# A decoder's nine layer norms fed without their centring product, after output weights and biases are centred once on the chip

## The chip, the cores and the metric

The kernel runs on one core of one Trainium2 chip. The metric is the device time of one launch in microseconds. Five engines work on a core, each with its own queue in program order: TensorE (PE, matrix products into the accumulation memory PSUM), VectorE (DVE), ScalarE (ACT), GpSimd (POOL) and SyncE (SP, which here issues the transfers). They wait for one another through semaphores.

## The reference, cut to what matters

32 sequences of 128 tokens with 128 features, and for each a context of 77 rows with 64 features, pass through a decoder of four levels (L0 to L3). A level has self attention, cross attention to the context, and a feed-forward part (a mixture of experts, a small linear map, or a stack of attention and MLP layers). The norm after each part is

```python
def _layernorm(x, axis=-1, eps=1e-05):
    m = jnp.mean(x, axis=axis, keepdims=True)
    v = jnp.var(x, axis=axis, keepdims=True)
    return (x - m) / jnp.sqrt(v + eps)
```

and it is applied to the sum of the part's input and its output: `x = norm(x + attention(x) @ Wo + bo)`. Some inner norms have a gain and a shift as well. The map of `L2_ffn` has a ternary weight: each element of W is rounded to -s, 0 or s by the mean absolute value s of W. In cross attention of L0 and L3 there is one head and no output matrix: the output is `softmax(q k) v`, with `v = ctx @ Wv + bv`.

## The kernel before, in words

All is kept transposed: a tile is 128 features (on the partitions) by 512 columns, four sequences of 128 tokens, f32. A loop of four turns takes a *group* of 8 sequences, as two *chains* (c = 0 and 1) of four. Ahead of the loop is a setup: SP loads the small weights (one tile `small`), POOL makes masks and identities, DVE makes `center` (the identity minus 1/128) and `average` (1/128), an output bias for two of the attentions, and the ternary weight `tern`; two small products on PE serve it (lines 429 to 465).

A norm (29 in a group, for each of the two chains) is a chain of six steps, and since the features lie on the partitions, a mean over them needs a matrix product:

1. `centre`, line 549, PE: `center` times the residual sum, into a PSUM bank: x minus its mean.
2. `square`, line 982, ACT: the square of that bank, into `sq` in SBUF.
3. `variance`, line 557, PE: `average` times `sq`, into another bank.
4. and 5. `inverse_deviation`, lines 991 and 994, ACT: logarithm of the variance plus eps, then exp(-0.5 of it), into `part`.
6. `apply`, lines 1229 to 1243, DVE: the centred bank times `part`, and gain and shift where there are any.

A product of f32 tiles is two instructions on PE, so a count of products is half of the count in a row.

The order of work is written out by hand on each engine. Between two stages lie the norms. The generator `front` yields after each part of a norm and after each part of the next stage's head (its first products); `crossing` advances the generators of the two chains in turn, and the stages call `step(second)` and `step(then)` at fixed places in their own bodies. So in the last item of self attention (`mha`, item t = 9) the first chain's centring product is issued ahead of the last `attend` (line 731 or 721), and its variance product behind it, ahead of the second chain's output product (line 753). After cross attention (`xattn`) and after the linear map (`linear`) both chains do their norms together (`close`).

PSUM has eight banks. `Banks.take` hands them out from rings, each ring in turn: `flow` goes round all eight, `scores` banks 0 to 3, `turned` and `head` 4 and 5, `attend` 6, `wide` 7. Whoever takes a bank waits for the event named as `freed_by` by the tenant before it. A centred tile frees its bank when the norm is applied, a variance tile when its logarithm is taken. `norm_rings` says from which rings a norm takes its two banks: in front of self attention the second chain's centred tile gets `attend` and its variance `wide`, and a first norm of the first chain gets `flow`, or `scores` after self attention.

`warm(n)`, line 542, issues n products without use, 128x512 in bf16, that keep PE at work in places where it would idle. Line 601 are the q and k products of a self attention head, 784 those of cross attention, 859 the router's logits, 829, 876 and 883 the first products of MLP and experts, 846 and 910 the second ones, 938 the product with `tern`.

Of the kernel before, what the change touches and what calls it, by code (L numbers as in the profile page):

```python
# [14 lines left out]
ALU = mybir.AluOpType  # L15
ACT = mybir.ActivationFunctionType
AX_X = mybir.AxisListType.X

P = 128
BATCH = 32  # L20
CTX_LEN, CTX_DIM = 77, 64
# [82 lines left out]
def sequence():  # L104
# [3 lines left out]
    seq = []  # L108

    def norm(name, src, after, dst, **k):  # L110
        seq.append(dict(kind="norm", name=name, src=src, after=after, dst=dst, eps=1e-5, g=None, add=None, behind=None) | k)
        return ("normed", name)
# [22 lines left out]
    e = norm("L0_xattn_ln", "u", e, "x")  # L135
    e = moe("L0_ffn", "x", e, shared=True, act=ACT.Gelu_apprx_tanh, glu=False, on="logits")
    e = norm("L0_ffn_ln", "u", e, "x")
    for i in range(DEPTH):
        n = f"L1_{i}"
        y = "x" if i == 0 else "y"  # L140
        e = norm(n + "_ln1", y, e, "hn", g=n + "_ln1")
# [7 lines left out]
    e = norm("L1_xattn_ln", "u", e, "x")  # L149
# [3 lines left out]
    e = norm("L2_attn_ln", "u", e, "x")  # L153
    e = norm("L2_ln1", "x", e, "y", g="L2_ln1")
# [14 lines left out]
    e = norm("L2_ffn_ln", "u", ("residual", "L2_ffn"), "x")  # L169
    e = mha("L3_attn", "x", e, "x", "u", mask="far", rel=True, bias=True, bo="L3_attn_bo",  # L170
            wiped="L2_a2")
    e = norm("L3_attn_ln", "u", e, "x")
    e = xattn("L3_xattn", e)
    e = norm("L3_xattn_ln", "u", e, "x")
    e = mha("L3_ffn", "x", e, "x", "u", bo="L3_ffn_bo")
    e = norm("L3_ffn_ln1", "u", e, "y", g="L3_ffn_ln1", eps=1e-6)
# [104 lines left out]
def decoder(nc, io, known):  # L281
# [17 lines left out]
    with ExitStack() as ctx:  # L299
# [32 lines left out]
        const_v = sb("const_v", [P, 2])  # L332
        out_bias = {n: sb("out_bias_" + n, [P, 1]) for n in ("L2_attn", "L3_attn")}
# [53 lines left out]
        setup_step = ctx.enter_context(nc.semaphore("setup_step"))  # L387
        setup_sum = ctx.enter_context(nc.semaphore("setup_sum"))

        with nc.Block() as block:  # L390
# [32 lines left out]
            def _(dve):  # L423
# [7 lines left out]
                nc.vector.memset(average[:], 1.0 / P)  # L431
                nc.vector.memset(average64[:], 1.0 / CTX_DIM)
# [13 lines left out]
                link(nc.vector.tensor_tensor(const_v[:, 1:2], W("L3_rel_v")[:, 0:1], W("L3_attn_bv"), ALU.add))  # L446
                dve.wait_ge(setup_sum, 2)
                for i, n in enumerate(out_bias):
                    nc.vector.tensor_tensor(out_bias[n][:], psum[1][:, i:i + 1], W(n + "_bo"), ALU.add)
# [5 lines left out]
                nc.vector.tensor_tensor(tern[:], tern[:], tern_neg[:], ALU.subtract)  # L455

            @block.tensor
            def _(pe):
# [4 lines left out]
                pe.wait_ge(setup_step, 5)  # L463
                for i, n in enumerate(out_bias):
# [56 lines left out]
        with nc.Fori(0, BATCH // GROUP) as g:  # L521
            with nc.Block() as block:

                @block.tensor
                def _(pe):
# [19 lines left out]
                    def centre(st, c, ring):  # L545
                        n, rows, w = st["name"], st.get("rows", P), st.get("cols", TOK)
                        pe.wait_ge(*input_of(st["after"], c))
# [422 lines left out]
                def _(act):  # L970
# [8 lines left out]
                    def square(st, c):  # L979
                        n, rows, w = st["name"], st.get("rows", P), st.get("cols", TOK)  # L980
                        act.wait_ge(*have("centred", (n, c)))
# [873 lines left out]
```

## Time and profile before

| | before |
|---|---|
| median of 3 runs | 5704.05 us (5701.13 to 5717.39) |
| the profiled execution's own time | 5674.14 us |
| its span in the profile | 5672.6 us |
| mean granted PE clock | 0.962 |
| PE busy | 5110.4 us, 90% |
| PE weight loads | 2613.1 us, 46% |
| ACT busy | 3051.5 us, 54% |
| DVE busy | 2829.6 us, 50% |
| POOL busy | 23.6 us, 0% |
| transfers | 15 GB/s in the mean |

The profile is of one execution, 30 us shorter than the median of the runs. Its four turns of the loop take 1405 to 1420 us each and repeat one pattern, so one group is read closely and multiplied by four. Busy time of PE is modelled at its ends and holds the filler products. An idle time in a row, in brackets, names what ended it.

### The profile page before, as it was taken

To read this page: it belongs to the slowest core of one execution; us is meant where nothing else is said; L and a number is where in the kernel's file an instruction comes from. 1 tells how busy PE (TensorE), PEld (TensorE's weight loads), DVE (VectorE), ACT (ScalarE), POOL (GpSimd) and SP (SyncE) were. 2 spreads that over 40 slices of the span, in tenths; PEclk is the share of its full clock that TensorE was granted. 3 is DMA by queue.
4 is the path that set the end of the run, shared out by engine and by line. 5 is a ranking of instruction groups with operands and counts; after the bars stand their busy time and mean duration, and the time that the engine had idled before them with its cause. 6 is when DMAs were issued, how large, how long until landed. Compare 5 with 4: busy or idle time off the path is not lost. (4 is left out here: it accounts for less than half of the span.)

```text
span 5672.6 us, 81045 instructions
## 1 busy us (share of the span) xinstructions
PE 5110.4 (90%) x27990; PEld 2613.1 (46%) x27990; DVE 2829.6 (50%) x6564; ACT 3051.5 (54%) x11252; POOL 23.6 (0%) x34
## 2 busy tenths in 40 slices
PE   7999988889799998888889999888898999989889
PEld 4444445544444444554344444455434444445443
DVE  5255555562525555556253545555625255555562
ACT  5444565564544456656454445665645444466564
POOL 0000000000000000000000000000000000000000
PEclk9989999999999999999999989999999999999999
DMA  1100000000010000000001000000000100000000
GB/s 37 41 6 6 18 18 12 5 1 15 25 41 6 6 21 18 9 5 1 19 25 37 6 6 20 18 9 5 1 19 22 41 6 6 23 16 9 5 1 19
DMA packets 22511, 85.93 MB, mean 15 GB/s; under 512 B 2512, under 2 KB 3024, under 8 KB 21968
## 3 DMA queue, kind: packets, MB, share of 16 engines
q1 hardware_dynamic: 22096, 80.58, 4.4%
q8 instruction: 238, 3.90, 0.3%
q14 instruction: 177, 1.45, 0.1%
HBM read 78.47 MB, written 2.10 MB: 14 GB/s over the span
## 5 line engine op out<-in xcount | busy, mean ns | idle before, releaser
L1051 ACT ACTIVATE work<-bank,rowmax 128x128 f32<-128x128 f32 (+1 forms) x4096 | 1395.1, 395 | 306.7 <-DVE rowmax L1366 305.9
L1051 ACT ACTIVATION_READ_ACCUMULATOR work<-bank,rowmax 128x1 f32 x4096 | 989.1, 244 | 0.0
L1366 DVE TENSOR_REDUCE rowmax<-bank 128x4 f32<-128x512 f32 (+2 forms) x1152 | 610.8, 578 | 458.8 <-PE bank L677 346.6
L694 PE MATMUL bank<-ident,work 128*128 128x128 f32 (+1 forms) x4096 | 658.2, 289 | 134.5 <-DVE probsT L1425 101.9
L542 PE MATMUL bank<-mask_causal,identb 128*128 128x512 bf16 x2368 | 676.3, 394 | 40.1 <-issue 28.7
L694 PEld LDWEIGHTS bank<-ident,work 128*128 128x128 f32 (+1 forms) x4096 | 488.6, 148 | 349.1 <-DVE probsT L1425 172.5
L1164 ACT ACTIVATE work<-bank,small 128x512 f32<-128x512 f32 x544 | 371.8, 688 | 490.1 <-PE bank L883 490.1
L910 PE MATMUL bank<-work,slot 128*128 128x512 f32 x1344 | 611.7, 592 | 0.0
L1621 DVE SCALAR_TENSOR_TENSOR part<-bank,small,sq 128x512 f32<-128x512 f32 x192 | 144.1, 751 | 785.0 <-PE bank L910 775.4
L1425 DVE COPY probsT<-bank 128x512 f32<-128x512 f32 (+2 forms) x832 | 479.6, 600 | 68.7 <-PE bank L694 64.9
L677 PE MATMUL bank<-km,q 32*128 32x512 f32 (+2 forms) x1792 | 426.2, 570 | 19.3 <-ACT work L1051 11.9
L910 PEld LDWEIGHTS bank<-work,slot 128*128 128x128 f32 x1344 | 254.7, 190 | 294.5 <-issue 288.7
L542 PEld LDWEIGHTS bank<-mask_causal,identb 128*128 128x128 bf16 x2368 | 224.7, 101 | 270.4 <-issue 151.7
L991 ACT ACTIVATE part<-bank,eps 128x512 f32<-128x512 f32 (+1 forms) x232 | 157.5, 679 | 334.7 <-PE bank L557 334.2
L982 ACT ACTIVATE sq<-bank 128x512 f32<-128x512 f32 (+1 forms) x232 | 136.9, 590 | 363.0 <-PE bank L549 362.6
L731 PE MATMUL bank<-probsT,vm 128*32 128x128 f32 (+1 forms) x6144 | 273.3, 286 | 49.4 <-ACT probsT L1065 36.6
L731 PEld LDWEIGHTS bank<-probsT,vm 128*32 128x32 f32 (+1 forms) x6144 | 188.1, 113 | 201.8 <-issue 154.0
L883 PE MATMUL bank<-x,slot 128*128 128x512 f32 x576 | 265.2, 603 | 0.0
L1076 ACT ACTIVATE spreadT<-bank 128x128 f32<-128x128 f32 (+3 forms) x352 | 138.1, 392 | 228.0 <-PE bank L707 228.0
L557 PE MATMUL bank<-sq,average 128*128 128x512 f32 (+1 forms) x464 | 249.0, 627 | 12.1 <-DVE x L1229 8.7
L876 PE MATMUL bank<-x,slot 128*128 128x512 f32 x512 | 239.4, 609 | 21.5 <-DVE work L1609 21.5
L883 PE MATMUL bank<-y,slot 128*128 128x512 f32 x512 | 235.7, 601 | 7.2 <-ACT work L1164 7.2
(266 smaller groups left out, 6226.6 us busy)
## 6 DMA issues: line engine op xcount, KB each, us to landing
slot<-in_w_stream SPq DMA_DIRECT2D x68, 512.0 KB, 3.4
slot<-in_w_stream SPq DMA_DIRECT2D x32, 768.0 KB, 3.9
slot<-in_w_stream SPq DMA_DIRECT2D x32, 384.0 KB, 3.1
small<-in_w_small SPq DMA_DIRECT2D x1, 2288.0 KB, 9.0
x<-in_x SPq DMA_DIRECT2D x8, 256.0 KB, 3.6
out<-x SPq DMA_DIRECT2D x8, 256.0 KB, 2.0
ctx<-in_ctx SPq DMA_DIRECT2D x8, 77.0 KB, 3.4
```

The costliest lines, as they stand in the source:

```text
L542: nc.tensor.matmul(b[:], identb[:], mask["causal"][:].unsqueeze(1).to_broadcast([P, 4, P]), start=True, stop=True)
L557: nc.tensor.matmul(b[0:rows, 0:w], (average if rows == P else average64)[:], B["sq"][c][0:rows, 0:w], start=True, stop=True).then_inc(*mad ...
L677: nc.tensor.matmul(banks.where(("scores", n, c, s, r))[:, 0:J * nk], B["q"][c][g32, s * P:(s + 1) * P], km[c][g32, s, 0:J, 0:nk], start=no ...
L694: ins = nc.tensor.transpose(b[0:nk, j * P:(j + 1) * P], probs[t % 2][:, r, j, 0:nk], ident[:])
L731: ins = nc.tensor.matmul(b[g32, 0:P], vals[c][0:nk, s, j, g32], pr[0:nk, r, j, :], start=(j == 0), stop=(j == J - 1))
L876: nc.tensor.matmul(b[:, 0:TOK], W(f"{base}_{w}_{e}")[:, m * P:(m + 1) * P], src, start=True, stop=True).then_inc(*made(lab, (n, e, c, m)))
L883: nc.tensor.matmul(b[:, 0:TOK], W(f"{base}_W1_{e}")[:, m * P:(m + 1) * P], src, start=True, stop=True).then_inc(*made("hid_raw", (n, e, c, ...
L910: ins = nc.tensor.matmul(b[:, 0:TOK], w[:, m * P:(m + 1) * P], hid[c][:, m, :], start=(m == 0), stop=(m == M - 1))
L1051: ins = nc.scalar.activation(probs[t % 2][:, r, j, 0:nk], banks.where(("scores", n, c, s, r))[:, j * nk:(j + 1) * nk], ACT.Exp, bias=rowma ...
L1164: nc.scalar.activation(hid[c][:, m, :], banks.where(("hid_raw", n, e, c, m))[:, 0:TOK], st["act"], bias=W(base + "_b1")[:, 4 * e + m:4 * e ...
L1366: V.tensor_reduce(m[:, 4 * r:4 * r + J], banks.where(("scores", n, c, s, r))[:, 0:J * nk] .rearrange("p (j k) -> p j k", j=J), AX_X, ALU.m ...
L1425: ins = V.tensor_copy(out, raw)
```

## The change

Six output matrices (the value matrix in the two cross attentions that have no output matrix) and five biases are centred over the output features in the setup: the mean of each row of the weight is subtracted on DVE, and the biases are multiplied by `center` on PE. Five products with one column each and the wait for the weights stand ahead of the two that were there. The ternary weight is centred as well. After that the sum of a normed x and such an output has mean zero over the features before it is normed. Nine of the 29 norms are marked `centred`: `L0_xattn_ln`, `L1_0_ln1`, `L1_xattn_ln`, `L2_attn_ln`, `L2_ln1`, `L2_ffn_ln`, `L3_attn_ln`, `L3_xattn_ln` and `L3_ffn_ln1`. For these `centre` issues nothing and takes no bank, `square` reads the residual sum in SBUF as soon as it is written, and `apply` multiplies from SBUF. `L1_0_ln1` and `L2_ln1` take the output of the norm just before. The other 20 norms are as they were. The yields stay, so the places of all other instructions do too.

```diff
-    e = norm("L0_xattn_ln", "u", e, "x")
+    e = norm("L0_xattn_ln", "u", e, "x", centred=True)
...
+        centred_weights = ["L0_xattn_Wv", "L1_xattn_Wo", "L2_attn_Wo", "L3_attn_Wo", "L3_xattn_Wv", "L3_ffn_Wo"]
+        centred_biases = ["L2_attn_bo", "L3_attn_bo", "L0_xattn_bv", "L3_xattn_bv", "L3_ffn_bo"]
+        wmean = sb("wmean", [P, len(centred_weights) + 1])
...
+                nc.vector.memset(wmean[:], 0.0)
...
                 link(nc.vector.tensor_tensor(const_v[:, 1:2], W("L3_rel_v")[:, 0:1], W("L3_attn_bv"), ALU.add))
+                for i, name in enumerate(centred_weights):
+                    rows = CTX_DIM if name.endswith("Wv") else P
+                    ins = nc.vector.tensor_reduce(wmean[0:rows, i:i + 1], W(name, rows), AX_X, ALU.add)
+                link(ins)
+                link(nc.vector.tensor_scalar(wmean[:, 0:len(centred_weights)], wmean[:, 0:len(centred_weights)], 1.0 / P,
+                                             None, ALU.mult))
+                for i, name in enumerate(centred_weights):
+                    rows = CTX_DIM if name.endswith("Wv") else P
+                    ins = nc.vector.tensor_scalar(W(name, rows), W(name, rows), wmean[0:rows, i:i + 1], None, ALU.subtract)
+                ins.then_inc(weights_centred, 1)
                 dve.wait_ge(setup_sum, 2)
+                for i, name in enumerate(centred_biases):
+                    ins = nc.vector.tensor_copy(W(name), psum[2][:, i:i + 1])
+                link(ins)
...
-                nc.vector.tensor_tensor(tern[:], tern[:], tern_neg[:], ALU.subtract)
+                link(nc.vector.tensor_tensor(tern[:], tern[:], tern_neg[:], ALU.subtract))
+                link(nc.vector.tensor_reduce(tcol[:, 0:1], tern[:], AX_X, ALU.add))
+                link(nc.vector.tensor_scalar(tcol[:, 1:2], tcol[:, 0:1], 1.0 / P, None, ALU.mult))
+                nc.vector.tensor_scalar(tern[:], tern[:], tcol[:, 1:2], None, ALU.subtract)
...
                 pe.wait_ge(setup_step, 5)
+                pe.wait_ge(weights_centred, 1)
+                for i, name in enumerate(centred_biases):
+                    nc.tensor.matmul(psum[2][:, i:i + 1], center[:], W(name), start=True, stop=True)
                 for i, n in enumerate(out_bias):
...
                     def centre(st, c, ring):
                         n, rows, w = st["name"], st.get("rows", P), st.get("cols", TOK)
+                        if st["centred"]:
+                            return
...
-                        act.wait_ge(*have("centred", (n, c)))
-                        nc.scalar.activation(B["sq"][c][0:rows, 0:w], banks.where(("centred", n, c))[0:rows, 0:w],
+                        act.wait_ge(*(input_of(st["after"], c) if st["centred"] else have("centred", (n, c))))
+                        src = B[st["src"]][c] if st["centred"] else banks.where(("centred", n, c))
+                        nc.scalar.activation(B["sq"][c][0:rows, 0:w], src[0:rows, 0:w],
                                              ACT.Square).then_inc(*made("squared", (n, c)))
...
-                        cen = banks.where(("centred", n, c))[0:rows, 0:w]
+                        cen = (B[st["src"]][c] if st["centred"] else banks.where(("centred", n, c)))[0:rows, 0:w]
```

## Rows read from the trace of the kernel before

**Rows 1.** The page, part 1: busy time, share of the span and instructions of each engine.

```profile
PE 5110.4 (90%) x27990; PEld 2613.1 (46%) x27990; DVE 2829.6 (50%) x6564; ACT 3051.5 (54%) x11252; POOL 23.6 (0%) x34
```

**Rows 2.** Who waited for whom: engine, tile and line, releaser, us in total, times, longest.

```profile
ACT sq L982 <- PE bank L549: 362.6, 216, 4.6
```

**Rows 3.** Timeline of the setup: start us, us, engine line op out<-in xcount [idle before <-releaser].

```profile
10.49 0.28 DVE L442 TENSOR_REDUCE tcol<-small 128x1 f32<-128x128 f32 x1
...
11.33 1.01 PE L465 MATMUL bank<-const_v,small 128*128 128x1 f32 x4
```

**Rows 4.** Timeline of `L0_xattn_ln` of group 0, both chains.

```profile
122.86 2.09 PE L549 MATMUL bank<-u,center 128*128 128x512 f32 x4
...
124.03 0.60 ACT L982 ACTIVATE sq<-bank 128x512 f32<-128x512 f32 x1 [2.27 <-PE bank L549]
```

**Rows 5.** Timeline of the tail of `L3_ffn`, group 0.

```profile
1280.83 1.02 PE L549 MATMUL bank<-u,center 128*128 128x512 f32 x2
...
1280.92 0.60 ACT L1065 ACTIVATE probsT<-bank 128x512 f32<-128x512 f32 x1 [5.49 <-PE bank L694]
...
1281.87 1.08 PE L731 MATMUL bank<-probsT,vm 128*32 128x128 f32 x32
```

**Rows 6.** Timeline of `L1_xattn_ln`, group 0, second chain's centring product and what follows it.

```profile
629.86 0.68 DVE L1229 TENSOR_TENSOR x<-bank,part 128x512 f32<-128x512 f32 x1
...
630.96 0.95 PE L859 MATMUL bank<-small,x 128*128 128x8 f32 x8
```

**Rows 7.** Timeline of `L2_attn_ln` and `L2_ln1`, group 0.

```profile
814.52 0.60 ACT L982 ACTIVATE sq<-bank 128x512 f32<-128x512 f32 x1 [1.54 <-PE bank L549]
...
816.40 0.69 ACT L991 ACTIVATE part<-bank,eps 128x512 f32<-128x512 f32 x1 [0.42 <-PE bank L557]
...
822.37 0.69 ACT L991 ACTIVATE part<-bank,eps 128x512 f32<-128x512 f32 x1 [0.26 <-PE bank L557]
```

**Rows 8.** Timeline of the start of `L1_0`, group 0, first chain's q and k.

```profile
272.76 1.93 PE L601 MATMUL bank<-hn,slot 128*64 128x512 f32 x4
```

**Rows 9.** Timeline of `L2_ffn_ln` and the start of `L3_attn`, group 0.

```profile
1077.62 0.69 DVE L1647 TENSOR_TENSOR u<-bank,x 128x512 f32<-128x512 f32 x1 [2.17 <-PE bank L938]
...
1083.07 1.12 PE L557 MATMUL bank<-sq,average 128*128 128x512 f32 x2 [2.16 <-DVE x L1229]
...
1084.89 1.88 PE L601 MATMUL bank<-x,small 128*128 128x512 f32 x4
```

**Rows 10.** Timeline of `L1_3_ln2`, group 0.

```profile
542.00 0.49 DVE L1243 TENSOR_SCALAR hn<-hn,small 128x512 f32<-128x512 f32 x1
...
542.63 1.95 PE L549 MATMUL bank<-y,center 128*128 128x512 f32 x2 [2.12 <-DVE hn L1243]
```

**Rows 11.** Timeline of `L1_attn_ln`, group 0, second chain, and the head of `L1_xattn`.

```profile
563.86 1.12 PE L549 MATMUL bank<-u,center 128*128 128x512 f32 x2 [0.71 <-DVE u L1532]
...
565.69 1.02 PE L601 MATMUL bank<-x,small 128*128 128x512 f32 x2
```

**Rows 12.** Timeline of `L2_a2_ln3`, group 0, TensorE alone.

```profile
1050.19 1.98 PE L829 MATMUL bank<-hn,slot 128*128 128x512 f32 x4
```

**Rows 13.** Windows: us, busy us (xcount) of the five engines, granted clock, DMA share, GB/s.

```profile
266.60:321.80 55.20, 50.64 (x266) 27.44 (x267) 34.70 (x111) 22.92 (x92) 0.00 (x0) 0.81 0.01 3
488.80:537.60 48.80, 43.30 (x270) 23.52 (x268) 34.36 (x112) 21.42 (x90) 0.00 (x0) 1.00 0.03 9
1194.80:1198.00 3.20, 1.09 (x4) 0.26 (x3) 1.17 (x2) 2.04 (x6) 0.00 (x0) 1.00 0.03 5
1198.00:1208.50 10.50, 10.36 (x31) 6.32 (x32) 3.86 (x9) 2.23 (x7) 0.00 (x0) 0.51 0.00 0
```

**Rows 14.** Lines by shape: engine op operands xcount | busy us, mean ns | idle before.

```profile
L994 ACT ACTIVATE part<-part 128x512 f32<-128x512 f32 x224 | 141.0, 630 | 7.2
...
L982 ACT ACTIVATE sq<-bank 128x512 f32<-128x512 f32 x224 | 133.6, 596 | 356.1 <-PE bank L549 356.1
...
L1627 DVE TENSOR_TENSOR u<-u,part 128x512 f32<-128x512 f32 x152 | 105.2, 692 | 5.2
```

More of the change, by code:

```diff
@@ L110, in norm @@
     def norm(name, src, after, dst, **k):
-        seq.append(dict(kind="norm", name=name, src=src, after=after, dst=dst, eps=1e-5, g=None, add=None, behind=None) | k)
+        seq.append(dict(kind="norm", name=name, src=src, after=after, dst=dst, eps=1e-5, g=None, add=None, behind=None,
+                        centred=False) | k)
         return ("normed", name)
@@ L140, in sequence @@
         y = "x" if i == 0 else "y"
-        e = norm(n + "_ln1", y, e, "hn", g=n + "_ln1")
+        e = norm(n + "_ln1", y, e, "hn", g=n + "_ln1", centred=i == 0)
         e = mha(n, "hn", e, y, "y", D=16, mask="causal", linear=True, bo=n + "_bo")
@@ L148, in sequence @@
     e = mha("L1_xattn", "x", e, "x", "u", nk=CTX_LEN, kv="ctx", kv_after=("ctx_loaded", ""))
-    e = norm("L1_xattn_ln", "u", e, "x")
+    e = norm("L1_xattn_ln", "u", e, "x", centred=True)
     e = moe("L1_ffn", "x", e, shared=False, act=ACT.Silu, glu=True, on="logits")
@@ L152, in sequence @@
     e = mha("L2_attn", "x", e, "x", "u", mask="causal", bias=True, bo="L2_attn_bo")
-    e = norm("L2_attn_ln", "u", e, "x")
-    e = norm("L2_ln1", "x", e, "y", g="L2_ln1")
+    e = norm("L2_attn_ln", "u", e, "x", centred=True)
+    e = norm("L2_ln1", "x", e, "y", g="L2_ln1", centred=True)
     e = norm("L2_a1_lnx", "y", e, "hn", g="L2_a1_lnx", g2="L2_a1_lny", dst2="hn2")
@@ L168, in sequence @@
     seq.append(dict(kind="linear", name="L2_ffn", src="x", after=e))
-    e = norm("L2_ffn_ln", "u", ("residual", "L2_ffn"), "x")
+    e = norm("L2_ffn_ln", "u", ("residual", "L2_ffn"), "x", centred=True)
     e = mha("L3_attn", "x", e, "x", "u", mask="far", rel=True, bias=True, bo="L3_attn_bo",
             wiped="L2_a2")
-    e = norm("L3_attn_ln", "u", e, "x")
+    e = norm("L3_attn_ln", "u", e, "x", centred=True)
     e = xattn("L3_xattn", e)
-    e = norm("L3_xattn_ln", "u", e, "x")
+    e = norm("L3_xattn_ln", "u", e, "x", centred=True)
     e = mha("L3_ffn", "x", e, "x", "u", bo="L3_ffn_bo")
-    e = norm("L3_ffn_ln1", "u", e, "y", g="L3_ffn_ln1", eps=1e-6)
+    e = norm("L3_ffn_ln1", "u", e, "y", g="L3_ffn_ln1", eps=1e-6, centred=True)
     e = moe("L3_ffn_moe", "y", e, shared=False, act=ACT.Gelu, glu=False, on="probs")
@@ L387, in decoder @@
         setup_step = ctx.enter_context(nc.semaphore("setup_step"))
+        weights_centred = ctx.enter_context(nc.semaphore("weights_centred"))
         setup_sum = ctx.enter_context(nc.semaphore("setup_sum"))
```

## The prediction

> **What bounds the kernel now.** I began with the page's busy shares [rows 1]: TensorE (PE) is busy 90% of the span, DVE and ACT about half. That doesn't make every matmul worth its time. Many PE instructions are fillers on L542, and each norm is a chain in which the engines take turns: residual (DVE), centring product (PE), square (ACT), variance product (PE), logarithm and exponential (ACT), multiplication (DVE). The list of waits shows the link that the change cuts: ACT waited 362.6 us in 216 instances for L549 [rows 2], 1.68 us each. 72 of the 232 centring products go (9 norms x 2 chains x 4 groups). By that mean they would be worth 121 us, but most chains run in pairs, or behind other work. So I read the nine places in the timeline one by one, in group 0, for what ends last, and used the windows for PE's granted clock.
>
> **The setup** is ahead of the loop and nothing covers it. Now two one-column products take 1.01 us and a 128x128 reduction 0.28 us [rows 3]. Added: six reductions, one small scaling, six subtractions on DVE, then five more products behind the last of them, five small copies, and a reduction, a scaling and a subtraction on the ternary weight. Products: 5 x 0.5 = 2.5 us. DVE pieces, each between 0.15 (overlapped) and 0.28 us: 13 before the products, 8 after, 3.1 to 5.9 us. Together 5.6 to 8.4 us; I take 6.1, near the lower end, since independent DVE instructions overlap. Once per run.
>
> **The centring product on the path**, per group. A product of this shape starts 122.86 and its square at 124.03 [rows 4]: 1.17 us from written input to square, which now starts at once.
> - `L0_xattn_ln` and `L3_xattn_ln`: both chains run together behind cross attention, so the pair saves one latency: 1.2 each, 2.4.
> - Four norms follow self attention (`L1_xattn_ln`, `L2_attn_ln`, `L3_attn_ln`, `L3_ffn_ln1`). There the first chain's product sits in PE's queue ahead of the last attend: 1280.83, attend at 1281.87, while the probabilities it needs are ready at 1280.92 + 0.60 = 1281.52 [rows 5]. Saved 0.3 in each. In the second chain nothing waits for its square, which is early, but the next stage's first product is queued behind the centring: x is ready at 629.86 + 0.68 = 630.54, the product starts 630.96 [rows 6]: 0.4 more in `L1_xattn_ln` and, by the same pattern, in `L3_attn_ln` (0.5). Without `L2_attn_ln`: 0.7 + 0.8 + 0.3 = 1.8.
> - `L2_attn_ln` with `L2_ln1`: the second chain's square is at 814.52, the two logarithms that follow in turn at 816.40 and 822.37 [rows 7]. The square can start when u is written, 1.2 earlier, and 0.3 from the tail; its variance no longer queues behind the first chain's second centring, nor does `L2_ln1`'s. I get 814.7 and 820.6 for the logarithms: 1.8, of which the 0.3 is part.
> - `L1_0_ln1`: q and k start at 272.76 [rows 8], behind the second chain's centring and four fillers; without it the variances go 0.6 earlier and hn is ready at 272.0: 0.75.
> - `L2_ffn_ln`: here a PSUM bank decides. The second variance (1083.07) waits 2.16 us until DVE has normed the first chain [rows 9], because its bank was last the first chain's centred tile. That tile is gone. u of the second chain is written at 1077.62 + 0.69 = 1078.31; square, the first chain's logarithm (0.69), exponential (0.63) and multiplication (0.69) end at 1081.1, and q starts there instead of 1084.89: 3.8 here, 4.0 to 4.1 where the first variance ran late too. I take 4.0.
>
> Sum of these: 2.4 + 1.8 + 1.8 + 0.75 + 4.0 = 10.75 us.
>
> **Banks that rotate.** The rings hand out banks in turn, so every dropped take shifts all later ones. I counted the takes of a group through. One wait goes: `L1_3_ln2` of the second chain starts its centring at 542.63, only after hn of the first is done at 542.49 [rows 10]; without it the products behind start 0.9 earlier. Two come. The second centring of `L1_attn_ln` (563.86) lands in the bank of the first and waits for its norm, 565.3; q, now at 565.69 [rows 11], comes behind it and four fillers, at 567.0: +1.35. The second centring of `L2_a2_ln3` waits in the same way until hn is ready, and the products of 1050.19 [rows 12] come 0.9 later. Bounds: 0, where the bank is free in time, and 2.2, two latencies. Net +1.35 per group.
>
> **The clock.** PE's granted clock was 1.00 in 1194.8 to 1198.0, with PE busy 1.09 of 3.2 us, and 0.51 in the next 10.5 us [rows 13]: it falls to the lower level, 1.2 GHz of 2.4, after little work. The change takes work out of such places. By my working new stretches without a full matmul arise ahead of `L1_0` (2.4 us), `L1_xattn` (2.3), the router of `L1_ffn` (2.3), in `L2_ln1` (3.3), before `L2_a2_mlp` (2.1) and before `L3_ffn_moe` (3.1, only 8-column products in it); two go, at `L1_3_ln2` and `L2_ffn_ln`. What a fall costs: half of the time at the lower level where PE is alone on the path, some 1.5 us for a short one; less inside attention: `L1_0` took 55.2 us at 0.81, `L1_3` 48.8 at 1.00 [rows 13]. A fall in half of the stretches is 0.75 each: 6 x 0.75 - 2 x 0.9 = +2.7 per group. Ends: 0 and 6 x 1.5 = 9.
>
> **SBUF instead of PSUM.** Exponential, from SBUF, 630 ns; square, from PSUM, 596 ns [rows 14]: up to 0.034 more for a square, 0.4 per group; the multiplication I cost at nothing, between -0.1 and +0.1 us: an addition with both inputs in SBUF takes 692 ns, and the multiplication with one in PSUM 0.68 [rows 6, 14]. The Trainium skill, page "VectorE: DVE Perf Modes", its opening table of specifications, has VectorE closer to SBUF and ScalarE closer to PSUM: by that rule the square loses and the multiplication gains; the page has no figure, and the trace has only the 34 ns, between two functions.
>
> **Sum.** Per group -10.75 - 0.9 + 2.25 + 2.7 + 0.4 = -6.3; four groups -25.2; setup +6.1: -19.1 us. The profiled execution took 5674.1 us and would take 5655; it is 30 us faster than the median of the runs, 5704.05. I carry the difference over: 5685, -0.33%. Less than 0.3% (17 us) can hardly be told from no change here.
>
> **Rivals.**
> 1. *The clock charges nothing.* The stretches grow, but the fall depends on more than they. Then -25.2 - 10.8 + 6.1 = -30: 5674. For it: at 1083 PE idled 2.16 us and the clock stayed up; against it: the fall at 1198. The Trainium skill, "TensorE: Matmul & The Clock Gate", section "Why this matters for your kernels", speaks only of idle gaps between bursts as what throws the clock back; by that rule most of my stretches would be free. The trace has a fall after a stretch in which PE was a third busy, so it bears out more than the rule.
> 2. *The bank wait at `L2_ffn_ln` stays*, or another one takes its place: 1.2 there instead of 4.0, +11: 5696.
> 3. *The gains are hidden.* The other chain, or DVE's router and softmax work, is late anyway and half of the 10.75 is lost: +21: 5706, the same as before.
> 4. *Slower: the lower clock sticks.* If the three new stretches ahead of attention (`L1_0`, `L1_xattn`, `L2_a1`) put it down and its short products can't bring it back, each costs up to the 6.4 us between `L1_0` and `L1_3` [rows 13], 77 us over four groups. Against -30 without the clock that turns the result from a share of 40% on, and is slower by 0.3% from 60%; at 80% it gives +31: 5735. Against it: such stages come back to 1.00 in the rows of before.
> That the norm isn't fed from SBUF, or is wrong by needing the product still, has no support: each listed input is an affine map with centred output weights plus an already normed x.
>
> **How the numbers follow.** Forecast 0.55 (own range 5670 to 5700), rival 1 0.15, 2 0.12, 3 0.10, 4 0.08. Faster by over 0.3% (under 5687): 0.55 x 0.6 + 0.15 + 0.12 x 0.2 + 0.1 x 0.1 = 0.52. Slower (over 5721): rival 4 and a tail of 3, 0.09. The rest, 0.39, is within 0.3%. The range for 8 in 10 runs from a little below rival 1, for the better ends of the bounds, to a little beyond rival 3: 5656 to 5714.
>
> **What would show it.** In the profile after: 72 centring products (144 instructions) fewer; squares of the nine norms start within 0.1 us of their input; attention's last attend 0.3 earlier after its transposes; at `L2_ffn_ln` no wait of the second variance for DVE; new waits of a centring for DVE at `L1_attn_ln` and `L2_a2_ln3`, none at `L1_3_ln2`; the first loop filler at 20.7 instead of 14.6; the mean clock a little under 0.962. Wrong would be: a setup over 9 us, squares that wait for ACT's earlier work, a group that shortens by under 3 us at an unchanged clock, or a clock under 0.95.

## The result: slower by 0.65%

| | before | after |
|---|---|---|
| median of 9 runs each | 5693.44 us | 5728.83 us |
| ratio, 95% interval | | 1.0065 (1.0044 to 1.0085) |
| profiled execution, own time | 5674.14 us | 5716.56 us |
| mean granted PE clock in it | 0.962 | 0.948 |
| mean granted clock of all runs | 0.9576 (90 runs) | 0.9450 (9 runs) |

The 90 runs of the kernel before are those taken beside the experiments; a 91st, 5741 us in the chip's slower state, is left out here and in every mean.

The prediction was 5685 us, and the time lies outside its range. It was counted from a median of 3 runs, 5704; counted from the 5693 of this table, the same change would have given 5674. One of its signs of being wrong came, a clock under 0.95. The page's first part for the kernel after, against [rows 1]:

```profile
PE 5112.5 (89%) x27800; PEld 2627.4 (46%) x27856; DVE 2833.3 (50%) x6586; ACT 3051.8 (53%) x11252; POOL 23.6 (0%) x34
```

The weight loads are fewer by 134, as expected: 144 less for the dropped products, 10 more for the five products of the setup. Of the products themselves 56 more records are missing from the trace. PE has fewer instructions and as much busy time: it worked at a lower clock. The list of waits shows that the link that was to be cut is cut, 71 waits and 72 us of it, against [rows 2]:

```profile
ACT sq L1010 <- PE bank L576: 291.0, 145, 5.4
```

Timelines of the kernel after, in the order of the steps: setup; `L0_xattn_ln`; tail of `L3_ffn` with `L3_ffn_ln1`; `L1_xattn_ln` with its router; `L1_3_ln2`; `L1_attn_ln`; `L2_a2_ln3`; `L2_ffn_ln` (group 0, start us, us, engine line op).

```profile
12.95 1.26 DVE L461 TENSOR_SCALAR small<-small,wmean 64x128 f32<-64x128 f32 x6
14.36 2.26 PE L488 MATMUL bank<-small,center 128*128 128x1 f32 x10 [2.80 <-DVE small L461]
...
21.03 1.44 PE L567 MATMUL bank<-mask_causal,identb 128*128 128x512 bf16 x3 [3.56 <-PEq L395]
...
129.26 0.75 DVE L1541 SCALAR_TENSOR_TENSOR u<-bank,small,x 128x512 f32<-128x512 f32 x1 [2.08 <-PE bank L847]
130.05 0.63 ACT L1010 ACTIVATE sq<-u 128x512 f32<-128x512 f32 x1 [1.09 <-DVE u L1541]
...
1311.38 0.60 ACT L1093 ACTIVATE probsT<-bank 128x512 f32<-128x512 f32 x1 [5.32 <-PE bank L721]
...
1312.34 1.08 PE L758 MATMUL bank<-probsT,vm 128*32 128x128 f32 x32 [0.89 <-ACT probsT L1093]
...
639.37 0.68 DVE L1257 TENSOR_TENSOR x<-u,part 128x512 f32<-128x512 f32 x1
...
640.11 1.06 PE L886 MATMUL bank<-small,x 128*128 128x8 f32 x8 [1.38 <-DVE x L1257]
...
548.58 1.13 PE L576 MATMUL bank<-y,center 128*128 128x512 f32 x2 [0.84 <-DVE y L1486]
...
570.07 1.10 PE L576 MATMUL bank<-u,center 128*128 128x512 f32 x2 [2.26 <-DVE x L1257]
...
1079.05 1.10 PE L576 MATMUL bank<-z,center 128*128 128x512 f32 x2 [2.12 <-DVE hn L1271]
...
1108.25 0.69 DVE L1675 TENSOR_TENSOR u<-bank,x 128x512 f32<-128x512 f32 x1 [1.40 <-PE bank L965]
1108.97 0.63 ACT L1010 ACTIVATE sq<-u 128x512 f32<-128x512 f32 x1 [2.34 <-DVE u L1675]
...
1112.22 1.88 PE L628 MATMUL bank<-x,small 128*128 128x512 f32 x4
```

Squares start 0.03 to 0.04 us behind their input. At `L1_3_ln2` the second centring waits for its own y, no longer for hn as in [rows 10]; at `L1_attn_ln` it waits 2.26 us for the first chain's norm, and at `L2_a2_ln3` 2.12 us. At `L2_ffn_ln` the q product starts 3.28 us behind the second chain's u; by [rows 9] it had been 6.58.

Windows of the kernel after, against [rows 13] (us, busy us of PE, PEld, DVE, ACT, POOL, granted clock, DMA share, GB/s): the cross attention head behind `L3_attn_ln` in group 1 and the 4 us ahead of it; the score stage of `L3_attn` in group 1 and the 4 us ahead of it; the head of `L3_ffn_moe`; the stretch behind `L2_a2_ln3`; and from `L3_attn_ln` to `L3_xattn_ln` in group 2.

```profile
2626.00:2630.20 4.20, 2.16 (x5) 0.53 (x4) 2.71 (x7) 1.92 (x3) 0.00 (x0) 0.98 0.00 0
2630.20:2650.70 20.50, 18.26 (x50) 10.70 (x50) 6.05 (x13) 4.37 (x13) 0.00 (x0) 0.50 0.00 0
...
2537.00:2541.00 4.00, 1.84 (x11) 1.01 (x9) 3.93 (x10) 3.76 (x22) 0.00 (x0) 1.00 0.00 0
2541.00:2554.60 13.60, 13.59 (x62) 7.64 (x63) 7.93 (x21) 9.71 (x52) 0.00 (x0) 0.75 0.01 2
...
2729.00:2736.50 7.50, 7.50 (x16) 4.02 (x16) 3.18 (x17) 0.88 (x2) 0.00 (x0) 0.54 0.00 0
...
1074.17:1101.06 26.89, 23.26 (x51) 9.28 (x49) 6.78 (x11) 11.13 (x17) 0.08 (x1) 0.94 0.02 4
...
4043.67:4071.77 28.10, 23.75 (x76) 13.97 (x77) 9.18 (x17) 8.73 (x20) 0.00 (x0) 0.64 0.00 1
```

The kernel before over the last two of these stretches, at clock 1.00:

```profile
1045.40:1069.66 24.26, 21.86 (x51) 8.61 (x49) 6.77 (x11) 11.13 (x16) 0.09 (x1) 1.00 0.02 4
...
4019.53:4041.81 22.28, 17.86 (x82) 10.07 (x83) 9.11 (x17) 8.63 (x19) 0.00 (x0) 1.00 0.00 1
```

In group 2, shown here, before has no fall in the last stretch; in groups 0 and 3 it has one of 10.2 us (in group 0 that of [rows 13]) and takes 25.8 us.

So the kernel after has falls in new places (a *fall* is a stretch in which PE's granted clock is at its lower level). Over the execution PE was at its lower level, half of the full clock, for (1 - 0.948) x 2 x 5715 = 594 us; in before for (1 - 0.962) x 2 x 5672.6 = 431. By the granted clock of windows over all four groups, five stretches hold the whole difference: `L1_attn_ln` to `L1_xattn_ln`, `L2_a2_ln3` to `L2_xattn_ln`, `L2_ffn_ln` to `L3_attn_ln`, `L3_attn_ln` to `L3_xattn_ln`, and `L3_ffn_ln1` to `L3_ffn_ln2` have 206 us at the lower level where they had 41 in before; all the rest has 388 where it had 389.

**Time and clock together.** Every run has its own granted clock. Within one kernel the time falls by 45 us for each 0.01 of mean clock. (That is the slope over the 90 runs of before; the 6 to 12 runs of each other kernel give 32 to 55, so it serves for small differences of clock.) Put to the same clock (0.960) by that slope, before takes 5678 us and after 5661: at an equal clock the change gains 17 us with its setup paid. The clock is lower by 0.0126, and that is 57 us. So the question for the experiments is what lowers it.

### The profile page after: what moved, and what is told of

Same layout as the page of the kernel before. It is cut to its first block and busy times, and to the rows that moved or that the text cites. A ratio compares the mean times of both kernels' runs of the same rounds, so it can differ in the third digit from the quotient of the medians.

```text
span 5715.0 us, 80667 instructions
## 1 busy us (share of the span) xinstructions
PE 5112.5 (89%) x27800; PEld 2627.4 (46%) x27856; DVE 2833.3 (50%) x6586; ACT 3051.8 (53%) x11252; POOL 23.6 (0%) x34
## 5 line engine op out<-in xcount | busy, mean ns | idle before, releaser
L567 PE MATMUL bank<-mask_causal,identb 128*128 128x512 bf16 x2368 | 689.9, 401 | 40.7 <-issue 28.1
L584 PE MATMUL bank<-sq,average 128*128 128x512 f32 (+1 forms) x464 | 263.7, 662 | 18.3 <-ACT sq L1010 18.0
L1010 ACT ACTIVATE sq<-bank 128x512 f32<-128x512 f32 (+1 forms) x160 | 93.9, 587 | 291.2 <-PE bank L576 291.0
```

Of the source, the lines that this page charges most:

```text
L567: nc.tensor.matmul(b[:], identb[:], mask["causal"][:].unsqueeze(1).to_broadcast([P, 4, P]), start=True, stop=True)
L584: nc.tensor.matmul(b[0:rows, 0:w], (average if rows == P else average64)[:], B["sq"][c][0:rows, 0:w], start=True, stop=True).then_inc(*mad ...
```

## The experiments

In the table, "rings" means that a dropped bank take still moves its ring on, "fill" a set of filler products described below. A median is of 6 runs, of 12 for e1 to e4, e6 and e18; the clock is the mean over a kernel's runs. The ratio is to runs of before beside the same kernel. The kernels were timed in five sessions on four chips (e1 to e4, e5 to e8, e9 to e12, e13 to e16, e17 and e18), in which the median of before was 5680 to 5693 us; where two kernels of different sessions are compared, a few us are not to be read.

| kernel | median us | ratio to before, 95% | clock |
|---|---|---|---|
| e1 setup alone | 5704.0 | 1.0027 (1.0000 to 1.0054) | 0.956 |
| e2 after, rings | 5723.0 | 1.0055 (1.0027 to 1.0083) | 0.945 |
| e3 after, fillers in the dropped places | 5724.3 | 1.0060 (1.0038 to 1.0082) | 0.948 |
| e4 after, centring product kept, unused | 5722.7 | 1.0056 (1.0030 to 1.0083) | 0.950 |
| e5 before, fill 1 | 5631.8 | 0.9892 (0.9851 to 0.9932) | 0.972 |
| e6 after, fill 1 | 5651.6 | 0.9940 (0.9909 to 0.9972) | 0.962 |
| e7 before, fill 2 | 5604.3 | 0.9853 (0.9812 to 0.9894) | 0.980 |
| e8 after, rings, fill 2 | 5614.0 | 0.9867 (0.9824 to 0.9910) | 0.971 |
| e9 after, fill 2 | 5643.2 | 0.9931 (0.9904 to 0.9958) | 0.967 |
| e10 e8 and fillers at two norms of L3 | 5614.0 | 0.9874 (0.9846 to 0.9902) | 0.972 |
| e11 before, fill 3 | 5603.2 | 0.9865 (0.9838 to 0.9891) | 0.985 |
| e12 e10, fill 3 | 5577.5 | 0.9814 (0.9787 to 0.9842) | 0.984 |
| e13 e8 less `L2_attn_ln`, `L2_ln1` | 5590.9 | 0.9816 (0.9785 to 0.9847) | 0.977 |
| e14 e8 with these two alone | 5622.3 | 0.9882 (0.9847 to 0.9917) | 0.978 |
| e15 e8 with `L2_ffn_ln` alone | 5611.6 | 0.9861 (0.9830 to 0.9891) | 0.977 |
| e16 e12 less some fillers | 5572.6 | 0.9795 (0.9760 to 0.9830) | 0.983 |
| e17 e16 less the two | 5578.5 | 0.9817 (0.9779 to 0.9855) | 0.982 |
| e18 e2 less the two | 5712.5 | 1.0046 (1.0026 to 1.0065) | 0.948 |

### Setup, banks, missing products (e1 to e4)

e1 is the kernel after with no norm marked. The other three change what `centre` does for a marked norm:

```diff
                         if st["centred"]:
+                            banks.n[ring] = banks.n.get(ring, 0) + 1      # e2
+                            warm(4, ring)                                 # e3
+                            ...  wait for the input, take the bank, issue the product   # e4
                             return
```

> The weights and biases are centred in the setup, but no norm is marked: all 29 keep their centring product, so the loop is that of before. Measured so far: the loop starts 6.3 us later in the changed kernel, and the whole is 37 us slower. Theory A (the clock: the centring products dropped from the norms had also kept TensorE at work, and without them it runs at its lower level more often): +6 us, ratio 1.001, granted clock as before, 0.96. Rival C (the setup, or the changed values, cost more than the 6.3 us seen at the loop's start): up to +37 us, 1.006.

> The changed kernel, but each dropped take of a bank still moves its ring on by one (no product, no wait), so that all other tiles lie in the banks they had before. Theory B (the loss comes from the shifted banks: tiles that wait for a bank in new places, as at L1_attn_ln and L2_a2_ln3, and what idles behind these waits): those waits go, and with them most of the loss; under 5695 us where before takes 5693, clock back to 0.96. Theory A (clock through missing products): the waits go, worth 4 x 2.25 us less the 4 x 0.9 us that a wait gained, and the rest stays: 5715 to 5730 us, clock 0.94 to 0.95.

> The changed kernel with four filler products (128x512, bf16, results unused) in place of each dropped centring product, in the same bank, waiting for no input. Theory A: TensorE is at work where it was before, granted clock 0.96 or more, and the worked-out gains show: 5655 to 5685 us, 0.993 to 0.999 of before. Theory B gives about the same here, since the banks too are as before; the run with the rings alone tells the two apart. Rival D (operands in SBUF, or a norm that is no faster for it): clock 0.96, but 5700 us or more.

> The changed kernel, but the nine norms still issue their centring product, at its place, with its wait for the input and in its bank; nobody reads it, square and multiplication take the residual sum from SBUF. It differs from before in the setup and in the release of ACT and DVE alone. Theory A: granted clock 0.96 or more, and the part of the gains that came through ACT (the square 1.2 us earlier at L0_xattn_ln and L3_xattn_ln, L2_attn_ln, and 4 us at L2_ffn_ln, since its bank wait goes) stays: 5670 to 5695 us. Rival D: 5700 to 5730 us at an unchanged clock.

e1: ratio 1.0027, at clock 0.956; put to an equal clock it is 6 us above before. The setup costs what the loop's later start shows (its first filler at 21.0 us, not 14.6), and no more. e2: the waits went and the time did not, so theory B is not the whole. At an equal clock e2 gains 5 us on the kernel after, as its removed waits promise (5.4), but its mean clock is as low. e3 and e4: theory A falls in this form. With fillers in the dropped places (e3), or the products themselves back (e4), the clock came back from 0.945 only to 0.948 and 0.950. Their times lie in the range of rival D, but not at its unchanged clock: put to 0.960, e3 takes 5671 us and e4 5676, where before takes 5678 without the setup. None of these versions kept the clock of before.

The profiled executions, one of each kernel, show where. In before, after and e1 to e4 the clock falls in the linear attentions `L1_0` to `L1_3`, about 30 us behind their first norm, in some groups and not in others, though their instructions are the same each time. PE was at its lower level for 184 us in these four stages in before (over all groups), 181 in e1, 154 in the kernel after, 229 in e2, 273 in e3 and 277 in e4. So by these profiles they are no part of the loss of the kernel after itself; they are where e3 and e4 lost again what they had won. In the five stretches of the kernel after that had 206 us, e3 and e4 have 79 each, near the 68 of e1; in all the rest e3 has 529 and e4 494, where before has 389. Apart from `L1_0_ln1` ahead of the first of them, e3 and e4 change nothing about the linear attentions but their distance in time from earlier work. So a rival formed that had not been in the prediction: the kernel has weak places of its own, and which of them fall depends on when they come.

### Filling the weak places (e5 to e8)

```diff
+                            if st["linear"] and t == 3:      # fill 1: ahead of the wait for DVE's spread tile
+                                fill(b, 5)
...
+                        fill(b, 4 if c else 2)               # fill 2: fill 1, this ahead of a cross attention's q
...
+                        if c == 0:
+                            fill(b, 3)                       # fill 2: and this ahead of the router product
```

`fill` issues filler products into the bank that the next product is about to take, so no ring moves. The places of fill 1 in the trace of before (timeline of PE), 1.53 us idle, and the window behind it, with the clock at 0.50:

```profile
300.60 0.39 PE L707 MATMUL bank<-ident,spread 128*64 128x128 f32 x1 [1.53 <-DVE spread L1403]
300.79 0.63 PE L663 MATMUL bank<-mask_causal,identb 128*128 128x256 bf16 x2
...
300.60:324.50 23.90, 23.46 (x106) 12.59 (x106) 12.38 (x40) 6.47 (x30) 0.00 (x0) 0.50 0.00 1
```

> The kernel before, with five filler products in the one bank that TensorE is about to use, ahead of its wait for DVE's spread tile of item 3 in the four linear attentions L1_0 to L1_3; in the trace of before it idles there 16 times, 1.5 us each, and in 12 of the 16 the clock falls to the lower level just behind. Theory F (the clock falls behind stretches with little work, these 16 places are the largest charge of that kind in both kernels, and the changed kernel only meets them, by where its other falls put it in time, more often): most of these falls go. The 184 us at the lower level in these four stages cost about 0.4 us each: 5620 to 5650 us, clock 0.970 or more. Rival G (this idle time isn't what brings it down, or the fillers cost as much as they save): 5685 to 5700 us, clock 0.955 to 0.960.

> The changed kernel with the same five fillers at the same 16 places. Theory F: 5660 to 5680 us, clock 0.960 to 0.967; it stays slower than the kernel before with these fillers, by 20 to 45 us, because its own new falls (head of the cross attention behind L1_attn_ln, L2_a2_ln3, L3_attn, L3_xattn, head of L3_ffn_moe) remain. If the loss of the change lay wholly in the linear attentions, the two would differ by less than 10 us, or the changed kernel would be the faster. Rival G: 5720 to 5735 us.

> The kernel before with the fillers of the linear attentions and, in the bank of the product that follows, 2 and 4 ahead of the q product of each cross attention head (first and second chain) and 3 ahead of the first chain's router product. It is the control for the next kernel. In before these places idle for 0 to 2.2 us, so where there is no gap the fillers cost 0.2 us each: 5615 to 5655 us, clock 0.970 to 0.980.

> The changed kernel with each dropped bank take still moving its ring on, and with the same fillers as the control. Theory H (the change is a gain of 20 to 30 us at an equal clock, and what turned it is the clock alone): with the banks as before and the gaps filled where the centring product stood, the clock is within 0.003 of the control's, and it is faster than the control by 15 to 30 us: 5590 to 5635 us. Rival D (the gains are not there even with a full clock): no faster than the control. Rival K (the earlier release itself brings new falls wherever it opens a gap): clock lower than the control's by 0.006 or more, time equal or above.

e5: 61 us faster than before, inside the range of theory F; `L1_0` to `L1_3` have no fall any more. The first stage, windows of before and of e5 (each from the first chain's exponential of `L1_0_ln1` to that of `L1_0_ln2`):

```profile
270.61:326.63 56.02, 52.47 (x275) 28.21 (x275) 35.08 (x114) 21.65 (x90) 0.00 (x0) 0.79 0.00 1
```

```profile
270.67:317.99 47.32, 43.49 (x280) 23.87 (x280) 34.26 (x114) 21.53 (x90) 0.00 (x0) 1.00 0.00 1
```

e6 is 20 us slower than e5 by the medians and 27 by the means, and in neither do the linear attentions fall: the change has falls of its own. e7 is faster again. e8, expected 15 to 30 us under it, is 10 above it, which is hardly more than the noise of two sets of 6 runs, but at a clock lower by 0.009, which is clear of it: theory H failed as I had put it and rival K stands. Put to an equal clock, e8 is some 30 us below e7.

### Which falls belong to the change (e9, e10)

e9 is e8 without the moved rings; e10 is e8 with `warm(4, ring)` in the dropped places of `L3_attn_ln` and `L3_ffn_ln1`.

> The changed kernel as it is, its banks shifted, with the fillers of the linear attentions, of the cross attention heads and of the router. Against the kernel with the same fillers and the rings moved on (5614 us, clock 0.971) only the banks differ. Theory B, now for a part of the loss: the shifted banks cost two new waits (net 5 us) and the falls that come only with them (at the head of the cross attention behind L1_attn_ln, and behind L2_a2_ln3, in 4 of 4 groups): 5625 to 5645 us, clock 0.965 to 0.969. If the banks cost their waits alone: 5616 to 5622 us at clock 0.971.

> The changed kernel with rings moved on and the fillers (5614 us, clock 0.971), and four fillers more in the places of the dropped centring products of L3_attn_ln and L3_ffn_ln1. Theory A, for its part: the two falls at the head of L3_ffn_moe, there in 3 or 4 of 4 groups in every kernel whose places are empty, and in none with work in them, go: 4 x 2 to 3 us, 5600 to 5608 us, clock 0.973 to 0.976. If the missing products have no part in it: 5610 to 5620 us.

e9 is 29 us above e8: the shifted banks cost more than their waits (5.4), as expected. Without fillers the same difference, after against e2, is 6 us, with the clock at 0.945 in both, so the price is not a fixed one. The falls of e9 are where theory B has them, behind `L1_attn_ln` in 3 of 4 groups and behind `L2_a2_ln3` in all. Windows of e8, then of e9, from `L1_attn_ln` to `L1_xattn_ln` of group 0 and behind `L2_a2_ln3`:

```profile
543.96:610.64 66.68, 60.89 (x556) 38.45 (x557) 39.97 (x91) 51.59 (x290) 0.00 (x0) 0.97 0.02 6
...
1034.63:1058.89 24.26, 21.86 (x51) 8.61 (x49) 6.77 (x11) 11.13 (x16) 0.08 (x1) 1.00 0.02 4
```

```profile
542.54:614.16 71.62, 64.09 (x556) 39.59 (x557) 39.91 (x91) 51.71 (x291) 0.00 (x0) 0.93 0.02 6
1029.90:1056.79 26.89, 23.27 (x51) 9.27 (x49) 6.78 (x11) 11.14 (x17) 0.09 (x1) 0.94 0.03 4
```

e10 did as theory A says in the trace and not in the time: no fall at the head of `L3_ffn_moe` in any of the four groups (3 of 4 in e8), and the same 5614 us. By the means e10 is 2 us faster, with an uncertainty of 7, so the 6 to 14 us that were expected are neither shown nor excluded. Over the profiled executions of ten kernels, the groups with a fall at the places that the change makes weak:

| place | norms as before (before, e1, e5, e7) | after (after, e6, e9) | rings (e2, e8, e10) |
|---|---|---|---|
| cross attention head behind `L1_attn_ln` | 0 of 16 | 8 of 12 | 0 of 12 |
| behind `L2_a2_ln3` | 0 of 16 | 11 of 12 | 0 of 12 |
| score stage of `L3_attn`, second chain | 1 of 16 | 11 of 12 | 3 of 12 |
| cross attention head behind `L3_attn_ln`, not filled | 0 of 12 | 5 of 8 | 2 of 4 |
| head of `L3_ffn_moe` | 0 of 16 | 7 of 12 | 7 of 12 |

The first two come with the shifted banks alone. The last two come with the missing centring product: in before, it stood in the wait for x, and with fillers or the product in its place (e3, e4) the last two rows have no such fall in 8 groups, the third row one. In the last row the falls are missing in e10, which has fillers there, and in e9, which has none but those that e8 has too; why e9 is without them no run shows. In the last two rows the kernels with the norms as before are not free of falls either, but theirs come later and are shorter: in the cross attention in 10 of 12 groups, some 10 us behind the exponential of `L3_attn_ln` and for 7 to 10 us in place of 20; in `L3_ffn_moe` in 12 of 16, 12 us behind that of `L3_ffn_ln1` and for 3 to 7 us, where the kernel after has two falls of 7 to 10 us in sum.

### An equal clock (e11, e12, e16)

Fill 3 adds fillers where PE still idled, in both kernels:

```diff
+                        if n in ("L2_ln1", "L2_a1_lnx", "L2_ln2", "L2_a2_lnx", "L2_a2_lny"):
+                            fill(b, 2)                       # ahead of the variance product
...
+                                if r == 0 and D == 32:
+                                    warm(2, "wide")          # ahead of the transposes of an item
...
+                                        fill(b, 14)          # L1_ffn, second chain's first gate product
...
+                                    fill(b, 5)               # L3_ffn_moe, second chain's first product
```

> The kernel before with all these fillers (5604 us, clock 0.980) and more where TensorE still idles: 2 ahead of each variance product of the five norms around the attentions of L2, 2 ahead of each item's transposes in these attentions (idle there 0.6 to 1.3 us), 14 ahead of the second chain's first gate product of L1_ffn (idle 5.4 us) and 5 ahead of the second chain's first product of L3_ffn_moe (1.8 us). The control for the next kernel; if the fillers lie in idle time: 5570 to 5600 us, clock 0.985 or more; if they push the path, 5605 to 5640 us.

> The changed kernel with rings moved on, fillers in the two places of L3, and all the fillers of the control. Theory H (at an equal clock the change is worth 20 to 30 us with its setup paid): clock within 0.003 of the control's and 15 to 30 us under it. Rival K (the earlier release brings falls of its own that fillers at these places don't stop): clock lower by 0.005 or more, and the difference from the control under 10 us or the other way. Rival D (no gain at an equal clock): equal clock, less than 5 us between them, or slower by the 6 us of the setup.

> The changed kernel with rings moved on and all fillers, less those that lay on the path (ahead of the variance products of L2_ln1 and L2_a1_lnx, +5.7 us in four groups, and in the items of L2_a1's attention and most of L2_a2's, +3 and +4 us). The version with all of them took 5578 us. Expected 5565 to 5575 us, 0.978 to 0.980 of before, if the clock stays at 0.982 or more; 5580 to 5590 if the fillers taken out had held it up.

Here the two kernels have the same clock, 0.985 and 0.984, and the changed one is 26 us faster (28 by the means), within the 15 to 30 of theory H, rival D is out. So the change, with its rings moved on, is worth its worked-out gain once PE has work in the gaps. e11 itself is no faster than e7: its fillers raised the clock by 0.005 and took as much time on the path. e16, without the fillers ahead of two variances and in most items, has the lowest median of the study, 0.9795 of before; the means of e16 and e12 differ by 2 us, so which of the two is faster is not shown.

### One pair of norms, one norm (e13 to e15, e17, e18)

> The changed kernel with the rings moved on and the first set of fillers (5614 us, clock 0.971), with L2_attn_ln and L2_ln1 unmarked, so that they take 6.0 us per group again and not 4.8. Theory P (these norms, shorter by 1.2 us, put L2_a2's weak place at another time against the falls upstream, and it falls in 2 of 4 groups, some 38 us each): the stretch L2_a2_lny to L2_a2_ln3 is back at 364 to 376 us (four groups, now 386 to 389), and the kernel is at 5595 to 5610 us, clock 0.976 or more, although it gives up 5 us. Rival S (no single place: every new gap takes its share): 5615 to 5622 us, clock 0.971.

> The same with L2_attn_ln and L2_ln1 alone marked, beside the setup. At full clock this is +6 for the setup and -5 for the norms against the control (5604 us, clock 0.980). Theory P: 5615 to 5625 us, clock 0.974 to 0.977, L2_a2 at 385 us. Rival S: 5603 to 5608 us, clock 0.979 to 0.980.

> The same with L2_ffn_ln alone marked. At full clock: +6 - 16 = -10 us against the control (5604 us). A fall in the q and score stage of L3_attn, 20 or 26 us behind the norm, in 4 of 4 groups instead of 2 or 3, takes 1.6 us for a short one and 4.7 for a long one: theory P and S alike expect 5594 to 5608 us at clock 0.975 to 0.980. If the gain is wholly given back there: 5608 us or more.

> The fastest version (5573 us, clock 0.983), with L2_attn_ln and L2_ln1 unmarked. If the pair does harm through the clock in any surroundings: 5550 to 5565 us. If its harm was chance, or is cured by the fillers there: 5 us more, 5575 to 5582 us.

> The changed kernel with the rings moved on and no fillers (5723 us, where before took 5690), with L2_attn_ln and L2_ln1 unmarked. If the pair does harm: 5695 to 5708 us. If not: 5720 to 5735 us.

By time e13 and e14 did what theory P says: 23 us less without the pair, 18 more with it alone, against +5 and +1 at an unchanged clock. But the intervals overlap those of e8 and e7, and the profiled executions contradict its place: the stretch in `L2_a2` takes 389.5 us in e13 (389 in e8) and 366 in e14 (364 in e7). e18, without fillers, is 10 us under e2, between the two expectations and not clear of the noise. e17, with the most gaps filled, is 6 us above e16, in accord with the 5 us that the pair saves, but their intervals overlap too. So the pair's harm is not shown, only made likely with fill 2, and not by way of `L2_a2`. e15: 7 us above e7, where 16 less for its gain and 6 more for the setup should give 10 under it; the clock is lower by 0.003, and what this norm saves seems to be given back, though 7 us are within the noise of the two.

## Why the prediction was wrong, by its own steps

At full clock a stretch takes the same time in every group to within 0.1 us, so the terms can be read one by one as differences between kernels in groups without a fall, or, where every group has one, with falls of the same length (from the first chain's exponential of one norm to that of the next; us per group):

| step | predicted | measured |
|---|---|---|
| `L0_xattn_ln` | -1.2 | -1.15 |
| `L1_0_ln1` | -0.75 | -0.6 |
| wait gone at `L1_3_ln2` | -0.9 | -0.9 |
| wait new at `L1_attn_ln` | +1.35 | +1.4 |
| `L1_xattn_ln` | -0.7 | -0.5, at full clock (e11, e12) -0.9 |
| `L2_attn_ln` with `L2_ln1` | -1.8 | -1.2 |
| wait new behind `L2_a2_ln3` | +0.9 | +0.9 |
| `L2_ffn_ln` | -4.0 | -3.7 to -4.1, at full clock -3.3 |
| `L3_attn_ln` and `L3_xattn_ln` | -2.0 | -1.85 |
| `L3_ffn_ln1` | -0.3 | 0 |
| SBUF operands | +0.4 | in the others |
| sum without the clock | -9.0 | about -7.8 |
| clock | +2.7 | about +15 |

**Right:** the setup (6.1 predicted, the first loop filler 6.4 later), the banks (all three waits, each to 0.1 us, counted through), `L2_ffn_ln` with its bank wait (rival 2 is out), `L0_xattn_ln`, and by that the sum of local terms, to 1.2 us in 9. Rival 3, hidden gains, is out as well.

**Wrong in a small way:** the 0.3 in each norm behind self attention. I took the attend of [rows 5] to be late by the centring product, 0.35 us behind the probabilities. In the kernel after nothing stands ahead of it, and it starts at 1312.34, 0.36 behind 1311.38 + 0.60. That is the handover from ACT to PE; the product lay beside it and cost nothing.

**Wrong in size, and it decided:** the clock term, +2.7 per group in the sum. Measured +37 us, less 6.4 for the setup, plus 4 x 7.8 that were gained, leaves some 60 us, 15 per group. The step said: six new stretches, a fall in half of them, 0.75 each. Three things in it failed.

First, the places. Of the six, three fall in half or more of the groups of the kernel after: ahead of `L1_xattn` (2 of 4), before `L2_a2_mlp` (4) and before `L3_ffn_moe` (4). Ahead of `L1_0` and at the router of `L1_ffn` there is no new fall, and in `L2_ln1` one in 4 groups, as in before. Two that I hadn't listed, the score stage of `L3_attn` and the cross attention head behind `L3_attn_ln`, fall in 4 and 3 of 4.

Second, the price of one. The short fall behind `L2_a2_ln3` cost 1.7 us (26.9, against 25.2 in the one group of e6 that has none), near the 1.5 I had; but the cross attention takes 28.1 us instead of 22.3 where the clock stays down through it, and 25.8 where it has the short fall of before. [Rows 13] had the row for it, 10.5 us at 0.51 behind one short stretch, and I still priced a short fall.

Third, I treated the clock as a sum over the places that the change touches. The falls that the kernel after has more than before do lie there (206 us against 41). But e3 and e4 show that the sum doesn't hold the other way: with work put back in these places they had 79 us, and the falls in the rest of the program rose from 389 us to 529 and 494, in stages that the change leaves alone.

Rival 4, the lower clock sticking, named the right mechanism with 5735 us (measured 5729) and had 0.08; its place, ahead of `L1_0` and `L2_a1`, was wrong, and `L1_xattn` only a part. The bound of the clock term, "0 and 9 per group", was too narrow as well, since it allowed only for short falls.

The rule of the Trainium skill behind rival 1 ("TensorE: Matmul & The Clock Gate", section "Why this matters for your kernels"), that idle gaps between bursts are what throws the clock back, does not hold here in that form: the longest idle time ahead of the falls shown was 2.17 us, below the gap that the page names. Ahead of the falls in the cross attention head and in the score stage shown above PE had been busy 2.16 of 4.20 and 1.84 of 4.00 us. The same page, in "What's actually happening", says that the gate's timing is free of the kernel's start and differs from run to run; the runs agree: one and the same kernel before had mean clocks between 0.948 and 0.967, and times between 5648 and 5735 us.

**Open:** why the weak places of the unchanged stages fall more often once other norms are shorter. That they do rests on one profiled execution of each kernel (e3, e4, and e8 against e7 in `L2_a2`) and on the mean clocks, which agree. The mechanism, that the distance in time to an earlier fall decides, is argued and fits groups that repeat their falls, but no run here isolates it. A rival is untested: the same stretch may fall or not by when it comes in an execution, whatever fell ahead of it. And a last point is open: with the falls of the change cured in place (e3, e4), no unfilled version is faster than before.

## What to carry to other kernels

A product that can be taken out of a chain may still be what keeps TensorE's clock up: price the removal as the latency saved and, apart from it, as a fall of the clock in the stretch that follows, at that stretch's whole length. Putting the work back need not bring the clock back. Before judging a change of under 1%, fill the gaps of both versions and compare them at an equal granted clock; time against clock over the runs of one kernel gives the exchange rate (45 us per 0.01 here). And when a tile is dropped, move its ring on all the same: the shift of all later banks cost 29 us between e8 and e9, though only 6 us, within the noise, between e2 and the kernel after.

## What the runs showed of the hardware that was not expected

- Five filler products in an idle time of 1.5 us, at 16 places, made the kernel 61 us faster (e5), 1.1%. They cost nothing while the clock is up: at full clock `L1_3`, from norm to norm, takes 47.16 to 47.20 us with them (e5) and 47.21 without (before).
- At full clock the program repeats to 0.1 us per stretch; the scatter of 1.5% between runs of one kernel is the granted clock. The spread that remains about the line of time against clock is 3 us.
- A square takes 628 ns from SBUF and 596 from PSUM on ACT; the multiplication takes 689 and 690 ns on DVE. The Trainium skill, "VectorE: DVE Perf Modes", has ScalarE closer to PSUM, and the trace agrees; VectorE, which by the same page is closer to SBUF, shows no difference here. The prediction says that this page has no figure, and that is wrong. Further down the same page of the Trainium skill, section "The TRN2 errata — SBUF-src ops pay a fixed extra latency per instruction", a table gives ScalarE a fixed part of 224 cycles from SBUF and 172 from PSUM, and VectorE 58 and 120. By an estimate from that table the square would lose 43 ns and the multiplication gain 65; the trace has a loss of 32 and no gain.
